# Four loads per sample of a two-layer attention kernel wait for a group of small matmuls

## The reference, cut to what matters

```
layer 0: q, k = Wq y, Wk y                       (1x1 convolutions over channels)
         attn = softmax(q k^T / 16) per head      (8 heads, 32 x 32: channels against channels)
         o    = Wo (attn (Wv x)) + x, then a norm over the whole sample
layer 1: q, k, v = projections of y
         in chunks of 64 positions, 8 heads: softmax(q k^T / sqrt(32) + mask) v
         out  = (Wout ... ) * mask + layer 0, then a norm over positions for each channel
```

## Time and profile before

| | us |
|---|---|
| median of 3 runs | 1555.93 |
| the profiled execution | 1555.52 |
| its span, first to last instruction | 1553.6 |
| PE busy | 1476.3 (95%) |
| DVE busy | 1265.6 (81%) |
| ACT busy | 1131.2 (73%) |
| POOL busy | 434.4 (28%) |
| mean granted TensorE clock | 0.978 |

### The profile page before, as it was taken

One profiled execution on the slowest core, in us unless ns is written; L12 is line 12 of the kernel. 1 busy time (PEld: TensorE's weight loads), 2 busy tenths in 40 slices (PEclk: granted clock), 3 DMA queues, 4 the chain that ended last, 5 costly groups with the idle time before them and its releaser, 6 DMA issues.

```text
span 1553.6 us, 55059 instructions
## 1 busy us (share of the span) xinstructions
PE 1476.3 (95%) x24353; PEld 1264.0 (81%) x24353; DVE 1265.6 (81%) x1944; ACT 1131.2 (73%) x1966; POOL 434.4 (28%) x292
## 2 busy tenths in 40 slices
PE   8999999999999999999999999999999999999984
PEld 6888888788887888888887888878888788888873
DVE  4788888788887888878878888878878788787885
ACT  5768777677777768777777777767777677786864
POOL 1204223142331413314042241412324132240420
PEclk9999999999999999999999999999999999999997
DMA  6223232423323242322423324233242332324121
GB/s 218 80 90 97 97 108 87 129 81 119 100 93 107 82 144 83 103 97 83 143 85 97 102 88 134 83 111 103 79 127 78 118 108 84 117 76 138 43 83 55
DMA packets 96397, 157.29 MB, mean 101 GB/s; under 512 B 5408, under 2 KB 38304, under 8 KB 96032
## 3 DMA queue, kind: packets, MB, share of 16 engines
q1 hardware_dynamic: 96160, 153.78, 30.2%
HBM read 120.20 MB, written 33.55 MB: 99 GB/s over the span
## 4 chain that ended last, share of the span: by engine, by line
PE 94%; issue 3%; DVE 1%; ACT 0%; POOL 0%; ACTq 0%; POOLq 0%; DVEq 0%
PE pj_ps L317 47%; PE l_ps L317 13%; PE s_ps L351 7%; PE l_ps L432 7%; PE s_ps L365 6%; PE s_ps L337 6%; PE l_ps L449 2%; PE l_ps L475 2%; PE l_ps L469 1%; PE l_ps L478 1%; PE s_ps L506 0%; PE l_ps L457 0%; PE l_ps L440 0%; PE l_ps L463 0%; PE l_ps L500 0%
## 5 line engine op out<-in xcount | busy, mean ns | idle before, releaser
L1230 POOL TENSOR_TENSOR prob<-prob,row_inv 128x1024 f32<-128x1024 f32 x128 | 245.0, 1920 | 546.5 <-DVE row_inv L934 544.7
L317 PE MATMUL pj_ps<-y_hi,w_hi 128*128 128x512 f32 x522 | 219.4, 424 | 4.5 <-ACT q_s L646 4.5
L1247 POOL TENSOR_TENSOR o_sb<-o_sb,u_sb 128x1024 f32<-128x1024 f32 x60 | 155.6, 2604 | 177.4 <-ACT o_sb L691 175.8
L317 PE MATMUL pj_ps<-y_hi,w_lo 128*128 128x512 f32 (+1 forms) x522 | 205.0, 397 | 0.0
L317 PE MATMUL pj_ps<-y_lo,w_hi 128*128 128x512 f32 (+1 forms) x534 | 204.4, 390 | 0.0
L917 DVE TENSOR_REDUCE row_max<-s_ps 128x16 f32<-128x1024 f32 x128 | 155.7, 1216 | 20.6 <-PE s_ps L337 20.6
L930 DVE TENSOR_REDUCE row_sum<-prob 128x16 f32<-128x1024 f32 x128 | 155.6, 1216 | 11.2 <-ACT prob L668 9.3
L924 DVE TENSOR_TENSOR prob<-s_ps,row_max 128x1024 f32<-128x1024 f32 x128 | 156.7, 1224 | 4.4
L317 PE MATMUL pj_ps<-w_hi,y_hi 128*128 128x256 f32 x512 | 152.7, 298 | 1.8 <-ACT v_s L657 1.8
L657 ACT COPY v_s<-pj_ps 128x512 f32<-128x512 f32 x128 | 74.1, 579 | 109.0 <-PE pj_ps L317 109.0
L662 ACT COPY prob_t<-s_ps 128x512 f32<-128x512 f32 x256 | 136.6, 590 | 16.8 <-PE s_ps L351 16.8
(11 more groups left out here) (137 smaller groups left out, 3553.1 us busy)
## 6 DMA issues: line engine op xcount, KB each, us to landing
y_raw<-in_ctx SPq DMA_DIRECT2D x64, 512.0 KB, 5.0
yt_raw<-in_ctx_t SPq DMA_DIRECT2D x64, 512.0 KB, 4.0
x_raw<-in_x SPq DMA_DIRECT2D x64, 512.0 KB, 4.0
out_z<-o_sb SPq DMA_DIRECT2D x60, 512.0 KB, 4.8
mask_b<-in_mask SPq DMA_DIRECT2D x64, 256.0 KB, 3.4
out_z<-o_sb SPq DMA_DIRECT2D x8, 256.0 KB, 2.7
u_sb<-in_w SPq DMA_DIRECT2D x2, 512.0 KB, 5.7
w_sb<-in_w SPq DMA_DIRECT2D x1, 1024.0 KB, 10.8
```

Of the source, the lines that this page charges most:

```text
L317: last = mm(dst[:, cut], lhs, rhs[:, cut], start=i == 0, stop=i == len(todo) - 1)
L1230: nc.gpsimd.tensor_tensor(cut, cut, row_inv[:, b % 2, e, :].unsqueeze(2).to_broadcast([P, 2 * HEADS, CHUNK]), ALU.mult).then_inc(probs_don ...
L1247: nc.gpsimd.tensor_tensor(o_sb[:, :, cut], o_sb[:, :, cut], u_sb[:, :, cut], ALU.add).then_inc(z_done, 1)
```

## The change

SP's order is altered; no other engine's code is. In slots 4 and 12 SP waits until the value products of that slot are done (`av_ready`) before it issues what it has to load there. The transposed y load with q = 4 moves from slot 3 to slot 4, behind that wait. So in slot 4 transposed y, y and the mask come after the value products, and in slot 12 the mask. The store of slot 12 now comes ahead of the wait, and `load_y(n, 6)` moves from the head of slot 12 to the end of slot 11, behind the x load that already stood there.

```diff
+BEHIND_VALUES = (1, 3)
...
+            def values_done(n, b):
+
+                if exists(n, 4, b):
+                    sp.wait_ge(av_ready, count(n, 4, b))
+
             def body(n, first, last):
                 for s in range(SLOTS):
                     b, j = divmod(s, PAIRS)
+                    if not first and s in T_STORE:
+                        store(n - 1, T_STORE.index(s))
                     if j == 0:
-                        if not (last and b + 3 >= BLOCKS):
+                        if b in BEHIND_VALUES:
+                            values_done(n, b - 1)
+                        if s == S_GRAM[2] and not last:
+                            load_yt(n, 4)
+                        if not (last and b + 3 >= BLOCKS) and b != 3:
                             load_y(n, b + 3)
                         if not (last and b + 2 >= BLOCKS):
                             load_mask_b(n, b + 2)
-                    if not first and s in T_STORE:
-                        store(n - 1, T_STORE.index(s))
                     for first_slot, load in ((S_GRAM[0], load_yt), (S_X, load_x)):
                         q = s - first_slot + 2
                         if last and load == load_x:
                             q += 1
-                        if 2 <= q < 6 and not (last and q >= 4):
+                        if 2 <= q < 6 and not (last and q >= 4) and not (load == load_yt and q == 4):
                             load(n, q)
+                    if s == SLOTS - 5 and not last:
+                        load_y(n, 6)
```

## The result

The changed kernel takes 1500.63 us, the median of four runs (1499.77 to 1507.04), against 1554.79 us for the kernel before in the runs beside it (1550.08 to 1556.34). The ratio is 0.9666, with a 95% interval of 0.9631 to 0.97. The forecast was 1499 us. The profiled execution took 1499.77 us with a span of 1498.0 us, 55.6 us less than before.

What follows compares the result with a forecast made beforehand. PE bounds the kernel (94% of the chain), stopped by late instruction packets behind SP's data. 1555.5 - 48.8 (stops) - 16.5 (clock) + 5 (left in slot 4) + 4 (slot 6) = 1499 us; range 1486 to 1526.

Steps and rivals of the forecast that it cites:

- The rival by which the packets are late by themselves: PE's stops have another cause than the data, so the change only moves loads: 1555 us, chance 0.06.
- Stops removed: PE's 27 stops in the value products of slots 4 and 12 go: 43.4 + 5.4 = 48.8 us gained.
- Left in slot 4: Value products of slot 4: 0.35 us a sample still lost to a late packet or DVE's split, 5 us in all.
- The extrapolated packet start: Slot 4: with no data ahead, PE's instruction packet would begin about 0.6 us before the group, leaving 0.4 us of stop.
- Left in slot 12: Value products of slot 12: no stop left, with a margin of 2.3 us; 0.7 us of idle kept for the range.
- the 3.6 that I called free: Slot 12: the unhindered packet's place, 3.6 us ahead of the group, taken from an unbroken group at 939.96.
- Left in the scores of slot 6: Held loads delay the next instruction packet, stopping PE in slot 6's scores: 0.25 us a sample, 4 us in all.
- The clock: Stretches behind PE's longer stops: 11 drops to a lower clock go with the stops, 1.5 us each, 16.5 us gained.
- The tail: Last sample: most of slot 12's stop stays, stores 2 and 3 go out later; about zero, -1.3 to +2 us.

Runs made afterwards that it cites:

- the order alone: The change's new order of SP's issues without its two waits for the value products, compared with the kernel before: ratio 0.9777, 1521.8 us.
- the run that holds all slots: The change, with the loads of slots 0 and 8 also held behind their value products: ratio 0.9675 to the kernel before, 1502.2 us.
- slot 4 alone: Only the slot 4 part of the change, slot 12 in its order of before, compared with the kernel before: ratio 0.9881, 1539.3 us.

## Why the prediction was right

**The cause.** PE stopped because a 16 KB packet of its own instructions came late behind SP's data. In all twelve traces every break of more than 0.17 us inside a group of value products or scores, 275 in all, ends 1.2 to 1.6 us after such a packet has ended. The stop is at a fixed distance in the program and moves when the code moves, while the loads stay (the two shifts by 128); it shrinks when the data go out later (slot 4) or earlier (the store of slot 12 in the order alone); data in flight with no packet due cost nothing (slot 0, and the run that holds all slots). The rival by which the packets are late by themselves falls. The Trainium skill, Runtime: NRT & Kernel Launch, "Instruction fetch mechanics", gives room for 2048 instructions on PE and calls the cost of an edge mostly hidden. These runs disagree: a single packet that starts less than some 2.2 us ahead of its edge stops PE. That section's other sentence, two lines of 256 instructions, fits these runs, though none of them counts the lines.

**The terms.** Stops removed: 48.8 us forecast, 49.2 measured from start to start (29.0 in slot 4, 20.2 in slot 12), all of them but for what is left. Left in slot 4: 5 us forecast, 7.0 measured at the stop and 3.0 more at the wait for DVE's split. That split was to cost little, since it was ready at 4.7 us after the group's start by the earlier trace rows and PE was to come at 4.4. In fact PE's first matmul on it starts at 4.88 us however short the stop is, so at least 0.5 us a sample stays where 0.35 was taken. The extrapolated packet start of 0.6 us before the group was 0.75 to 1.0 in most samples. PE resumed 2.2 to 2.4 us behind it in the eight samples in which the packet took under 1.0 us, as in the rows, and 2.6 to 2.7 behind it in the seven in which it took 1.2 to 1.3 us, so those lose up to 0.7 us all the same. Left in slot 12: nothing, as forecast; the packet's lead there is 2.3 us, and that is enough. It isn't the 3.6 that I called free, though nothing holds it: the store has landed, and the DMA engines carry no packet at all from 541 us until this one starts at 543.5 (DMA view, 541.0 to 543.5):

```profile
DMA packets 0, 0.00 MB, mean 0 GB/s; under 512 B 0, under 2 KB 0, under 8 KB 0
```

So 3.6 us was no fixed free place; in sample 3 of the kernel before the packet started even 7.0 us ahead of the unbroken group. What lets it go earlier in those two samples, no run shows. The small wait behind an unbroken slot 12 wasn't counted; it now shows in all samples and costs 3.3 us more than before. Left in the scores of slot 6: 4 us forecast, none measured; the packet came 0.5 to 2.5 us later than before, and as PE reached the edge at 10.6 us and not at 10.2, the margin just sufficed. Left over in all 13.3 us against 9.

**The clock.** 16.5 us forecast; all 11 drops went, and by the stretches with and without one they had cost 17.0, so the term held. Its reasoning didn't hold in full: I took a drop as the price of any long stop. In the kernel before five of the 16 stops of 1.7 us of idle and more brought none. The order alone has 14 stops of 1.3 to 2.5 us without one drop, while slot 4 alone has 14 stops in slot 12 with five. A stop of that length may bring a drop or not, and no run shows what decides it. So it isn't shown that the change won these 17 us by taking away the stops, and that all 11 went was in part luck. The drops go with a wider spread of the kernel before: its medians were 1554.8 to 1559.8 us with single runs from 1544 to 1576, where the change's four lie within 7 us, and the mean clock on record was 0.985 in the run of 1544.5 us and 0.975 in that of 1575.8.

**The sum.** 1553.6 - 1498.0 = 55.6 us between the spans. The value products lose 42.2 us less (49.2 - 7.0) and the clock 17.0 less; against these stand 3.0 us for the split and 3.3 behind slot 12: 52.9. Some 2 us of the rest have nothing to do with the stops that I counted: 0.8 us up to sample 1, 0.3 in the tail, and 1.0 between slots 8 and 12 of the last sample, where the kernel before had one more drop of the clock. So the total is nearer to the forecast than its parts are: the forecast had 4.3 us too little for what is left over, and these 2 us and small differences in the other terms make up for it. That the profiled execution came within 1 us of the forecast is luck.

**The tail.** Forecast at zero: the stop behind matmul 86 is 2.77 us instead of 2.99, and ACT waits for stores in two places instead of one, 6.10 and 2.43 us:

```profile
1458.68 1.26 ACT L728 ACTIVATE o_sb<-l_ps,o_bias 128x512 f32<-128x512 f32 x2 [6.10 <-DMA out_z<-o_sb]
...
1464.29 1.27 ACT L728 ACTIVATE o_sb<-l_ps,o_bias 128x512 f32<-128x512 f32 x2 [2.43 <-DMA out_z<-o_sb]
```

From the start of the group to the end of the span it is 43.1 us (1454.88 to 1498.0) against 43.4 (1510.19 to 1553.6): no change.

## What to carry to other kernels

If PE stops inside a row of small matmuls on no semaphore, always at the same instruction, look in the DMA view for the instruction queue's packet just before it resumes, and for what your own queue has in flight then: a load that isn't needed soon can wait until the dense part is over, and one that is ready early should go out early, but look at the next packet too, since the held data move toward it. The gain is bound to the place of the code: any edit of PE's program before that point can put the edge elsewhere (128 instructions more, and the same change won nothing), so look again at the breaks after each one. And look at the wait that comes next behind a stop, as it may hide under it: here it kept 0.5 us a sample.

## What the runs showed of the hardware that I had not expected

- A shift of PE's code by 128 instructions, with nothing else changed that matters, moved 29 and 20 us of stops out of the value products and put 23 us into the scores of other slots; and on the changed kernel it costs 2.3 us a sample.
- PE resumes 1.2 to 1.6 us after the end of its instruction packet, in 275 breaks of twelve kernels. The packet takes 0.9 us at the least and up to 1.9 us, so PE resumes 2.2 us or more behind its start.
- Stops of PE of 1.3 to 2.5 us in 14 samples came without one drop of the clock, next to 11 drops in 27 stops of the kernel before.
- 64 tiny float32 matmuls as the profile counts them, of 32 columns, took 13.9 us at the very start, 0.22 us each.
- 256 KB in flight ahead of the packet lengthened the stop hardly at all (0.1 us a sample), 1.25 MB by 1.5 us.
